# A one-core kernel for a gated recurrent block and two MLPs: weight splits, a normalisation and taps in another order

## The reference, cut to what matters

```
t  = rmsnorm(x, norm1_w)
xb = conv4(t @ Wx)                          # causal depthwise, 4 taps, bias
r, i = sigmoid(xb @ Wa), sigmoid(xb @ Wi)
a  = exp(-8 * softplus(lam) * r)
h  = scan(a, sqrt(max(1 - a*a, 1e-12)) * i * xb)    # h[s] = a[s] * h[s-1] + b[s]
h1 = x + (h * gelu(t @ Wy)) @ Wo
u  = rmsnorm(h1, norm2_w)
x1 = layernorm(x + h1 + (gelu(u @ Wg) * (u @ Wu)) @ Wd)
out = layernorm(x1 + relu(x1 @ W1 + b1) @ W2 + b2)
```

## Time and profile before

| | us |
|---|---|
| median of 3 runs | 611.52 |
| lowest, highest | 611.2, 612.4 |
| the profiled execution | 612.55 |
| its span in the trace | 610.8 |
| TensorE busy | 596.2 (98%) |
| VectorE, ScalarE, GpSimd busy | 383.6, 312.0, 192.7 |
| mean granted clock of TensorE | 0.996 |

### The profile page before, as it was taken

How to read it: one execution, slowest core, us unless ns; L and a number is a source line. 1 busy time by engine, 2 the same in 40 slices (tenths; PEclk the granted TensorE clock), 3 DMA queues, 4 the chain that set the end, 5 groups by cost and what they waited for, 6 DMA issues and landing times.

```text
span 610.8 us, 9285 instructions
## 1 busy us (share of the span) xinstructions
PE 596.2 (98%) x3539; PEld 521.3 (85%) x3539; DVE 383.6 (63%) x699; ACT 312.0 (51%) x591; POOL 192.7 (32%) x289
## 2 busy tenths in 40 slices
PE   7999998999999999999999999999999999999996
PEld 6468786889898988889988898889988889989896
DVE  4778887274774747847585747748468464662565
ACT  5777944375444743465443753537443663322353
POOL 1263132314514072121724035131531305240131
PEclk9999999899999999999999999999999999999999
DMA  7521001000101001010100101000000100010011
GB/s 260 179 70 35 0 2 35 0 2 1 35 0 35 1 1 36 1 35 0 36 1 2 34 1 35 1 10 26 1 0 1 36 1 1 2 35 1 0 35 36
DMA packets 13100, 15.68 MB, mean 26 GB/s; under 512 B 616, under 2 KB 12288, under 8 KB 13056
## 3 DMA queue, kind: packets, MB, share of 16 engines
q1 hardware_dynamic: 13056, 15.09, 7.4%
HBM read 10.89 MB, written 4.19 MB: 25 GB/s over the span
## 4 chain that ended last, share of the span: by engine, by line
PE 87%; DVE 6%; issue 3%; POOL 2%; ACT 1%; DMA 0%; POOLq 0%; DVEq 0%
PE psum L337 16%; PE psum L339 16%; PE psum L338 16%; PE psum L348 10%; PE psum L350 10%; PE psum L349 10%; PE psum L355 3%; PE psum L390 2%; DVE xb L1037 1%; DVE row L1112 1%; PE psum L418 1%; PE psum L519 1%; PE psum L521 1%; PE psum L517 1%; POOL gu_hi L1468 1%
## 5 line engine op out<-in xcount | busy, mean ns | idle before, releaser
L1468 POOL TENSOR_SCALAR gu_hi<-gu_raw 128x512 fp32r<-128x512 f32 x64 | 52.1, 814 | 319.1 <-DVE gu_raw L1135 319.1
L1145 DVE TENSOR_TENSOR hid_lo<-hid_raw,hid_hi 128x512 fp32r<-128x512 f32 x56 | 45.4, 811 | 83.7 <-ACT hid_hi L846 83.7
L842 ACT ACTIVATE hid_raw<-psum,vecs 128x512 f32<-128x512 f32 x56 | 38.4, 686 | 114.5 <-PE psum L339 114.5
L1135 DVE TENSOR_TENSOR gu_raw<-psum,gu_raw 128x512 f32<-128x512 f32 x64 | 44.1, 689 | 74.3 <-PE psum L339 73.5
L348 PE MATMUL psum<-w_d_hi,gu_hi 128*128 128x256 f32 x256 | 72.9, 285 | 0.9 <-DVE gu_lo L1140 0.8
L348 PE MATMUL psum<-w_hi,hid_hi 128*128 128x256 f32 x256 | 71.8, 280 | 0.6 <-DVE hid_lo L1150 0.4
L350 PE MATMUL psum<-w_d_hi,gu_lo 128*128 128x256 f32 x256 | 71.9, 281 | 0.0
L350 PE MATMUL psum<-w_hi,hid_lo 128*128 128x256 f32 x256 | 71.9, 281 | 0.0
L349 PE MATMUL psum<-w_lo,hid_hi 128*128 128x256 f32 x256 | 71.8, 280 | 0.0
L349 PE MATMUL psum<-w_d_lo,gu_hi 128*128 128x256 f32 x256 | 71.7, 280 | 0.0
L833 ACT ACTIVATE gu_raw<-psum 128x512 f32<-128x512 f32 x64 | 38.1, 596 | 52.0 <-PE psum L339 51.5
(11 more groups left out here) (189 smaller groups left out, 1525.7 us busy)
## 6 DMA issues: line engine op xcount, KB each, us to landing
out_dram<-row SPq DMA_DIRECT2D x15, 256.0 KB, 2.2
xs<-in_L_attn_x_dram SPq DMA_DIRECT2D x7, 512.0 KB, 3.5
raw<-in_L_ffn_W_dram SPq DMA_DIRECT2D x2, 1024.0 KB, 7.3
raw_gud<-in_L_attn_Wg_dram SPq DMA_DIRECT2D x1, 1024.0 KB, 8.6
raw_gud<-in_L_attn_Wu_dram SPq DMA_DIRECT2D x1, 1024.0 KB, 10.7
raw_gud<-in_L_attn_Wd_dram SPq DMA_DIRECT2D x1, 1024.0 KB, 12.8
xs<-in_L_attn_x_dram SPq DMA_DIRECT2D x2, 256.0 KB, 2.9
raw_xyai<-in_L_attn_Wx_dram SPq DMA_DIRECT2D x1, 256.0 KB, 2.6
```

The source lines that it names most:

```text
L842: nc.scalar.activation(hid_raw[:, w % SLOTS, :], bank[:, :], ACT.Relu, bias=vec("b1", m)).then_inc(relu_ready, 1)
L1135: nc.vector.tensor_tensor(gu_raw[:, r % SLOTS, :], up_bank(r)[:, :], gu_raw[:, r % SLOTS, :], ALU.mult).then_inc(gu_ready, 1)
L1145: nc.vector.tensor_tensor(hid_lo[:, w % SLOTS, :], hid_raw[:, w % SLOTS, :], hid_hi[:, w % SLOTS, :].bitcast(FP32), ALU.subtract).then_inc ...
L1468: nc.gpsimd.tensor_scalar(gu_hi[:, r % SLOTS, :], gu_raw[:, r % SLOTS, :], 1.0, 0.0, ALU.mult, ALU.add).then_inc(gu_hi_ready, 1)
```

## The change

It edits five places.

- TensorE: the wait for tanh_a_ready and the four fillers ahead of first_out go; three fillers behind the first pair of u's transposes go. The waits for Wd's pieces become one piece in round 1, two in round 5.
- Wg and Wu: ScalarE makes both high pieces of Wg ahead of tanh_decay(0) and both of Wu behind gelu_y(0). VectorE makes w_g_lo's first piece ahead of squared_decay and its second ahead of the first add_mix; then it waits for rms2_rstd, once before the last tap there and once before w_u_lo.
- Wd: the high pieces move from GpSimd to ScalarE, one behind gelu_y(1), one to round 2. GpSimd adds x to h1 right behind first_rms.
- The table of the exponentials is loaded ahead of tanh_decay(1) in round 3.
- Chunk 0's ln_scale and normalise go from behind round 8's work and from round 9 to the head of round 8, and the third chunk's six taps go from rounds 9 and 10 to rounds 8 and 9.

```diff
@@ -599,11 +599,10 @@
             def first_period(r):
 
                 gate_up(r)
-                if r == 1:
-                    pe.wait_ge(hi_split["d"], pieces["d"])
-                    pe.wait_ge(lo_split["d"], 1)
-                if r == 5:
-                    pe.wait_ge(lo_split["d"], pieces["d"])
+                if r in (1, 5):
+
+                    pe.wait_ge(hi_split["d"], 1 + r // 5)
+                    pe.wait_ge(lo_split["d"], 1 + r // 5)
                 if 1 <= r < KH - 1:
                     down(r - 1)
                 if r == 3:
@@ -683,14 +682,12 @@
             pe.wait_ge(w_loaded["y"], DMA)
             raw_product(DOWN, "y", first_tT[0], wy_done)
             first_x(1)
-            pe.wait_ge(tanh_a_ready, KD)
-            keep_running(4, GATE)
             pe.wait_ge(w_loaded["o"], DMA)
             pe.wait_ge(tanh_i_ready, KD)
             first_out(SECOND)
             pe.wait_ge(gy_ready, KD)
             raw_product(DOWN, "y", first_tT[1], wy_done)
-            transposed_by_pairs(normed, 0, u_ready, uT_done, GATE, (3, 5))
+            transposed_by_pairs(normed, 0, u_ready, uT_done, GATE, (0, 5))
             for r in range(KH):
                 first_period(r)
             for r in range(KH, UNITS):
@@ -891,9 +888,12 @@
                 if r == 2:
                     weight_hi("x", "n1")
                     weight_hi("y", "n1")
+                    weight_hi("d", ks=[1])
                 if r == 3:
                     weight_hi("2", ks=[1])
                     square_x(2)
+
+                    act.preload_act_table(ACT.Exp)
                     tanh_decay(n)
                     exp_decay(n)
                     tanh_input(n)
@@ -967,7 +967,7 @@
             conv_start(0, 0)
             conv_start(0, 1)
             square_x(1)
-            weight_hi("g", "n2", ks=[0])
+            weight_hi("g", "n2")
             tanh_decay(0, bank=GATE)
             act.wait_ge(consts_ready, 1)
             exp_decay(0)
@@ -975,15 +975,14 @@
             gate_scale(0)
             act.preload_act_table(ACT.Gelu_apprx_tanh)
             gelu_y(0, bank=DOWN)
-            weight_hi("g", "n2", ks=[1])
-            weight_hi("u", "n2", ks=[0])
+            weight_hi("u", "n2")
             conv_start(1, 0)
             conv_start(1, 1)
             square_first_h1(0)
-            weight_hi("u", "n2", ks=[1])
             first_norm_u(0)
             split_hi_by_pairs(uT_hi, 0, GATE, uT_done, uT_hi_ready)
             gelu_y(1, bank=DOWN)
+            weight_hi("d", ks=[0])
             act.wait_ge(lo_split["g"], pieces["g"])
             for r in range(KH):
                 first_period(r)
@@ -1240,13 +1239,11 @@
                 p, m = divmod(r, KH)
                 n, f, s = p + 1, p - 1, p - 2
                 mixing, first, second = n < CHUNKS, 0 <= f < CHUNKS, 0 <= s < CHUNKS
-                if m == 1 and first:
+                if r == KH or m == 1 and f >= 1 and first:
                     normalise(f, 0, 0, x1_ready)
                     normalise(f, 0, 1, x1_ready)
                 if m == 2 and first:
                     split_lo(x1T_lo, x1T_hi, x1T_hi_ready, x1T_lo_ready, f)
-                if m == 2 and p == 1:
-                    convolve(n, 2)
                 if m == 3 and second:
                     second_sum(s)
                 if m == 4 and second:
@@ -1262,7 +1259,11 @@
                 if mixing:
                     if m == 0 and p >= 2:
                         split_lo(tT_lo, tT_hi, tT_hi_ready, tT_lo_ready, n - 2)
-                    if m == 1:
+                    if r == KH:
+                        convolve_half(n, 0, 0)
+                    if r == KH + 1:
+                        convolve_half(n, 1, 0)
+                    if m == 1 and p >= 2:
                         convolve(n, 0)
                     if m == 2:
                         xb_lo(n)
@@ -1278,10 +1279,14 @@
                 if units(r):
                     gate_lo(r)
                 if mixing:
-                    if m == 1:
+                    if r == KH:
+                        convolve_half(n, 0, 1)
+                    if r == KH + 1:
+                        convolve_half(n, 1, 1)
+                        convolve(n, 2)
+                    if m == 1 and p >= 2:
                         convolve(n, 1)
-                        if p > 1:
-                            convolve(n, 2)
+                        convolve(n, 2)
                     if m == 4:
                         room(n)
                 if m == 0 and f >= 1 and first:
@@ -1329,6 +1334,7 @@
             lam_stepped(nc.vector.tensor_scalar(z, lams, 0.0, -0.5 * C_CONST, ALU.max, ALU.mult))
             nc.vector.scalar_tensor_tensor(half_c[:, :], poly, -C_CONST, z, ALU.mult,
                                            ALU.add).then_inc(consts_ready, 1)
+            weight_lo("g", "n2", ks=[0])
             squared_decay()
             gated_input(0, [0])
             dve.wait_ge(tT_done, 4)
@@ -1338,11 +1344,14 @@
             gated_input(0, [1])
             scan_both(0)
             gated(0)
+            weight_lo("g", "n2", ks=[1])
             add_mix(0, 0, bank=SECOND)
             convolve_half(1, 0, 0)
             add_mix(0, 1, bank=SECOND)
+
+            dve.wait_ge(rms2_rstd, 1)
             convolve_half(1, 0, 1)
-            weight_lo("g", "n2")
+            dve.wait_ge(rms2_rstd, 2)
             weight_lo("u", "n2", ks=[0])
             split_lo_by_pairs(uT_lo, uT_hi, 0, GATE, uT_hi_ready, uT_lo_ready)
             weight_lo("u", "n2", ks=[1])
@@ -1468,13 +1477,6 @@
                 nc.gpsimd.tensor_scalar(gu_hi[:, r % SLOTS, :], gu_raw[:, r % SLOTS, :], 1.0, 0.0, ALU.mult,
                                         ALU.add).then_inc(gu_hi_ready, 1)
 
-            def weight_hi(n, norm=None, ks=None):
-                pool.wait_ge(w_loaded[n], DMA)
-                for k in range(pieces[n]) if ks is None else ks:
-                    nc.gpsimd.tensor_scalar(piece(flat(w_hi[n]), n, k), piece(raw_of[n], n, k),
-                                            vec(norm, k) if norm else 1.0, 0.0,
-                                            ALU.mult, ALU.add).then_inc(hi_split[n], 1)
-
             def round_of(r):
                 p, m = divmod(r, KH)
                 n, f, s = p + 1, p - 1, p - 2
@@ -1487,6 +1489,9 @@
                         first_rms(n, ss2, h1_squared, rms2_ms, rstd2, rms2_rstd)
                         add_x_h1(n)
                     return
+                if r == KH:
+                    for q in range(PAIRS):
+                        ln_scale(0, 0, q)
                 if mixing:
                     if m == 0:
                         head(n)
@@ -1494,7 +1499,7 @@
                         tail(n)
                 if r < UNITS:
                     gate_hi(r)
-                if m == 0 and first:
+                if m == 0 and f >= 1 and first:
                     for q in range(PAIRS):
                         ln_scale(f, 0, q)
                 if m == 3 and second:
@@ -1525,11 +1530,9 @@
             tail(0)
             head(1)
             first_rms(0, ss2, h1_squared, rms2_ms, rstd2, rms2_rstd)
-            weight_hi("d")
+            add_x_h1(0)
             tail(1)
             pool.wait_ge(b2_loaded, DMA)
-            add_x_h1(0)
-            pool.wait_ge(lo_split["u"], pieces["u"])
             for r in range(UNITS):
                 round_of(r)
             for q in range(PAIRS):
```

## The result

The changed kernel takes **604.59 us** (four runs, 604.51 to 604.64), the kernel before 611.95 us in the runs beside it (611.2 to 612.4). The ratio is 0.9881, 95% interval 0.9864 to 0.9898: 7.4 us less. The profiled execution took 604.58 us, its span is 602.8, where before it was 610.8. TensorE is still the bound.

A forecast was written before the change was run, and what follows sets the result against it. TensorE's matrix products bound the kernel from 111 us on, so gains come only before. Beginning 3.85 plus first x1 4.15 make 8.0 us: 604.5 profiled from 612.55, 603.5 for the median (before 611.52), range 602.7 to 606.0.

The forecast's parts named there:

- rivals 1 and 2: First (chance 0.14): clock falls once anyway, 605.1; second (0.12): VectorE and GpSimd collide more, 605.1, down to 606.
- up(11) late by: After mlp_up(0), up(11) waits for hid_hi(0) about 0.2 us, which the slow clock hid before.
- Fillers: Ahead of first_out on TensorE: removing four fillers gains 0.74 us, 0.9 without a collision, 0.4 with the full one.
- Waits for the rstd pairs: VectorE waits, so GpSimd's second pair costs 0.96 us, not 2.58; the wait costs nothing, without cover up to 0.5.
- Table: Loading the exponentials' table ahead of tanh, in ScalarE's idle time, gains 0.7 us around down(4) and down(5); bounds 0 and 0.75.
- First x1: 8th to 10th round: earlier x1 and taps gain 0.95 + 1.8 us; with the clock and small losses 4.15.
- The clock: Behind the gap ahead of mlp_up(0): with the gap cut to 0.4 us no fall to 1.2 GHz, gaining 1.6 us.
- Beginning: All gains ahead of the first x1: 3.1 us up to down(0) plus 0.7 for the table, 3.8 to 3.9.
- w_u_lo's 0.6 us: Ahead of u(0): TensorE's wait for w_u_lo, 0.43 us idle plus 0.15 restart, goes: 0.6 us gained.
- Ahead of down(0): VectorE free of w_d_lo, so TensorE's wait of 0.6 us with restart shrinks to 0.25: 0.35 gained, summed as 0.4.
- 0.95 for x1: x1 complete at 93.75 instead of just before 99.17, so its transposes don't wait: 0.83 idle plus 0.12 restart gained.
- 1.8 for the taps: Taps earlier let mlp_up(0) start at 103.8 instead of 106.58: 2.75 us, of which 0.95 is counted already.

The follow-up runs named there:

- a_fillers: The changed kernel with the wait for tanh and the four fillers put back ahead of first_out: span 603.6 us, 0.8 longer.
- a_nowait: The changed kernel without VectorE's two waits for rms2_rstd: span 603.4 us, 0.6 longer.
- a_begin: The changed kernel with rounds 8 to 10 as before (normalise, scales and taps back): 607.24 us, ratio 0.9928; one run of four at 608.42.
- b_again: The kernel before, unchanged, run ten more times: six from 611.12 to 611.27 us, four from 612.49 to 612.74; lower-level trace has span 609.5.
- b_rounds: The kernel before with only the change's edits for rounds 8 and 9 (ln_scale, normalise, six taps): 608.67 us, ratio 0.9947.
- a_taps_back: The changed kernel with only the third chunk's taps back in rounds 9 and 10, normalise kept at round 8's head: span 603.4 us, 0.6 longer.
- a_transposes: The changed kernel without the five fillers behind u's transposes: 604.62 us; four runs 604.69, 605.57, 604.49 and 604.55.

## Why the prediction was right, and where not

The measured 604.59 lies within 602.7 to 606.0, 1.1 above the 603.5 forecast. It is 0.2 outside the 602.8 to 604.4 that the forecast spanned by itself, and inside the range through the room left for rivals 1 and 2, neither of which came. Step by step, forecast and changed kernel's trace:

| step | forecast | trace |
|---|---|---|
| squared_decay | 21.4 | 21.20 |
| first_out | 30.47 | 30.31 |
| second rstd pair ready | 36.8 | 36.69 |
| gate_up(0) | 40.15 | 39.81 |
| w_u_lo's second half | 1.3 us | 1.80 us |
| down(0) | 46.0 | 46.16 |
| x1 complete, ahead of gate_times_up(8) | yes | yes |
| mlp_up(0) | about 100 | 99.92 |
| up(11) late by | 0.2 | 0.23 |
| profiled execution | 604.5 | 604.58 |

**Right.** Both places, their mechanisms, and what is late next in each. *Fillers*: 0.74 forecast, 0.85 measured by a_fillers; I had feared that gy would be later than it was. *Waits for the rstd pairs*: a_nowait shows the collision and that VectorE loses nothing. *Table*: 0.7 forecast, 0.9 measured. *First x1*, without the clock: 0.95 + 1.8 = 2.75 forecast; a_begin at its lower level has span 605.4 against 602.8, so 2.6. *The clock* in an execution that has the fall: 1.6, less the 0.2 for up(11) that the slow clock hid, so 1.4 forecast, 1.3 measured; without a fall up(11) waits in the kernel before too (0.24 in b_again), and both terms are nothing. *Beginning*: 3.85 forecast; the kernel before at its lower level has span 609.5, against a_begin's 605.4, so 4.1. 4.1 + 2.6 is the whole difference of 6.7 us between 609.5 and 602.8; by way of b_rounds, whose median span is 606.9, it is 2.6 for the first x1 and 4.1 for the beginning, the same. Within the beginning only four edits were taken back singly, and they give 0.8, 0.9, 0.6 and 0.2 us; the transposes' three fillers, ScalarE's order and Wd's move to ScalarE with the earlier addition were not.

**Wrong in size, in opposite directions.** Of w_u_lo's 0.6 us only 0.3 came: g(0) to u(0) was 2.09 us and is 1.80, as the addition of x to h1 still collides with it and GpSimd's copy of xtail waits behind it. Ahead of down(0) 0.26 came of 0.4; gate_up(0), 0.34 earlier than forecast, made up for most of both. And the split of 0.95 for x1 and 1.8 for the taps is in fact about 2.0 and 0.6 (a_taps_back, which takes the taps back with x1 moved); only their sum was right. That the profiled execution came out at 604.58 for 604.5 is in part luck: the beginning gave 4.1 for 3.85, the first x1 with the fall 3.9 for 4.15.

**The step that failed** is the one from the trace to the median: "I predict 604.5 for a profiled one and 603.5 for the median". The profiled execution of before was one in which the clock fell; I saw that the median was 1.0 us below it and carried this distance over. But the distance was the fall itself, which my sum had already booked as 1.6 us of gain. For an execution without the fall the gain is 6.7 us by the spans (609.5 to 602.8), for one with it 8.0 (612.55 to 604.58, as the sum said). b_again shows the two levels, 1.3 us apart. The three times given before hinted at them: 611.2 and 611.52 near the lower, 612.4 at the upper. Either way the changed kernel's time without a fall is the profiled one less the whole sum, 604.5, and that should have been the forecast for the median too. As a gain on the mean of executions, 1.6 and -0.2 together should have been 1.3 times the share at the upper level, which was 9 of 23 beside b_again and 4 of 7 beside b_rounds.

The rivals: none came. No fall of the clock was seen before 590 us in the changed kernel's trace nor in those of its variants (one run of a_begin, 608.42, has the lower mean clock); the one run of 605.57 (a_transposes) is unexplained. Collisions were there (normalisations 1.84 to 2.74 us, the 6-column copies 0.19 to 1.2) but lay mostly off the path.

## What to carry to other kernels

Before a term is booked as won, ask whether the profiled execution has something that the median has not: times at two levels beside one trace with a fall of the clock say that the term belongs to some executions only. On engines that hinder each other a wait can be a gain: VectorE waits 0.45 and 0.87 us for GpSimd's small scales and has them 0.6 us earlier. When work moves off a late engine, recompute the whole queue behind it: here x1 alone shortened the next round so far that the taps' move was worth a third of what its gap suggested.

## What the runs showed of the hardware

The same program with the same idle time of 2.17 us ahead of the same matmul kept TensorE at 2.4 GHz in one trace and fell to 1.2 GHz in another, from about 107.5 to 111 us (granted clock 0.57 over 107 to 111), at a price of 1.3 us. The first matmul behind the gap started at 106.58, 0.9 us ahead of the fall. A copy of 128x6 elements on GpSimd, 0.19 us alone, took 1.18 to 1.20 us when it was issued beside a VectorE instruction with two inputs from SBUF (w_g_lo at 30.62, w_u_lo at 39.67). In the one case (30.76) GpSimd came second and lasted as long as w_g_lo, which kept its 1.28; in the other w_u_lo came second, behind the addition, and was prolonged, to 1.80; the copy (40.32) came third and ended with it. The Trainium skill, SBUF — State Buffer, section "Who interferes with whom", says that the ports which the two engines share are an exclusive lock, and that the order of issue decides who blocks. The trace agrees.
